# The last eleven slots of a fused attention and expert kernel, written out by hand over three bank pairs

## What is computed

```python
q = xn @ Wq + bq;  latent = xn @ Wl + bl          # 16 heads of 8
k = latent @ Wk + bk;  v = latent @ Wv + bv
attn = softmax(q k^T / sqrt(8))                    # per head, 256 x 256
y_attn = (attn v) @ Wo + bo

f = batchnorm(xn @ fWq + fbq)                      # 8 heads of 32 = two halves of 16
s0, s1 = l2norm(half) . l2norm(sub_key)            # 32 scores for each half
ts0, ti0 = top4(s0);  ts1, ti1 = top4(s1)
w = softmax of the 16 sums ts0[i] + ts1[j];  expert = 32*ti0 + ti1   # clamped to 128 experts
y_ffn = sum_k up[expert_k] * w_k * gelu(down[expert_k] . xn)
out = x + y_attn + y_ffn
```

## Time and profile before

| | |
|---|---|
| median of 3 runs | 374.73 us (374.39 to 374.91) |
| the profiled execution | 377.74 us, its span 375.7 us |
| busy over the span: PE, DVE, ACT, POOL | 327.1, 329.2, 254.1, 255.1 us |
| mean granted TensorE clock | 0.968 |
| first second scores after slot 127, start | 344.21 us |
| last copy to ysb, start | 373.02 us |

### The profile page before, as it was taken

How to read it: one execution, slowest core, us unless ns; L and a number is a source line. 1 busy time by engine, 2 the same in 40 slices (tenths; PEclk the granted TensorE clock), 3 DMA queues, 4 the chain that set the end, 5 groups by cost and what they waited for, 6 DMA issues and landing times.

```text
span 375.7 us, 9660 instructions
## 1 busy us (share of the span) xinstructions
PE 327.1 (87%) x3080; PEld 175.1 (47%) x3080; DVE 329.2 (88%) x1407; ACT 254.1 (68%) x388; POOL 255.1 (68%) x544
## 2 busy tenths in 40 slices
PE   3999897976998898989898989898998989898874
PEld 2455553342354454544454545454454544454443
DVE  6599988789779999999999999999999999998561
ACT  3699967867566757667666676766757667667761
POOL 6388876706656777685867767677777675857870
PEclk9999996996599999999999999999999999999999
DMA  4664676029140403242141505050403130000100
GB/s 133 180 182 134 182 177 165 7 58 100 26 77 17 72 26 77 55 49 73 30 87 18 90 12 101 4 100 16 87 25 77 54 50 19 1 17 3 31 16 14
DMA packets 45886, 24.81 MB, mean 66 GB/s; under 512 B 5452, under 2 KB 45708, under 8 KB 45836
## 3 DMA queue, kind: packets, MB, share of 16 engines
q1 hardware_dynamic: 45836, 24.20, 30.3%
HBM read 15.54 MB, written 8.39 MB: 64 GB/s over the span
## 4 chain that ended last, share of the span: by engine, by line
PE 55%; DVE 24%; issue 8%; ACT 8%; POOL 4%; POOLq 0%; ACTq 0%; DVEq 0%
PE bank L590 12%; DVE negm L820 9%; PE bank L650 8%; PE bank L633 8%; PE SI L526 7%; DVE r_sb L885 6%; PE SJ L569 5%; PE SJ L607 2%; ACT s_sb L380 2%; PE bank L675 2%; POOL prod L1038 2%; PE bank L677 2%; PE bank L676 2%; PE bank L539 1%; PE SI L454 1%
## 5 line engine op out<-in xcount | busy, mean ns | idle before, releaser
L820 DVE TENSOR_REDUCE negm<-SI 128x4 f32<-128x1024 f32 x128 | 154.2, 1216 | 5.2 <-PE SI L526 5.0
L413 ACT ACTIVATE Eb<-SJ 128x1024 f32<-128x1024 f32 x128 | 130.6, 1020 | 32.3 <-PE SJ L569 32.2
L1038 POOL TENSOR_TENSOR prod<-r_sb,a 128x1024 f32<-128x1024 f32 x31 | 60.2, 1943 | 26.6 <-issue 25.8
L590 PE MATMUL bank<-Eb,vhat 128*18 128x256 f32 x1024 | 70.3, 394 | 0.0
L526 PE MATMUL SI<-KS,QS 48*128 48x256 bf16 x512 | 51.8, 281 | 15.5 <-DVE negm L820 14.6
L569 PE MATMUL SJ<-QS,KS 50*128 50x256 bf16 x512 | 51.7, 282 | 8.2 <-ACT Eb L413 8.0
L865 DVE MAX8 top<-s_sb 128x8 f32<-128x32 f32 x512 | 50.6, 180 | 4.9 <-ACT s_sb L380 4.9
L526 PEld LDWEIGHTS SI<-KS,QS 48*128 48x128 bf16 x512 | 18.2, 96 | 55.3 <-issue 43.5
L885 DVE MATCH_REPLACE8 r_sb<-top,s_sb 128x36 f32<-128x36 f32 x256 | 43.1, 180 | 0.0
L650 PE MATMUL bank<-cst,prod 128*128 128x128 f32 x256 | 34.5, 278 | 4.2 <-ACT s_sb L380 3.5
L633 PE MATMUL bank<-kblk,fqT 128*128 128x256 f32 x128 | 37.1, 413 | 0.5 <-ACT s_sb L380 0.4
(11 more groups left out here) (144 smaller groups left out, 585.9 us busy)
## 6 DMA issues: line engine op xcount, KB each, us to landing
qk_parts<-parts SPq DMA_DIRECT2D x48, 128.0 KB, 2.4
QS<-qk_parts SPq DMA_DIRECT2D x32, 96.0 KB
KS<-qk_parts SPq DMA_DIRECT2D x32, 96.0 KB
x_sb<-L_attn_x SPq DMA_DIRECT2D x8, 256.0 KB, 3.4
QS<-qk_parts SPq DMA_DIRECT2D x32, 64.0 KB
KS<-qk_parts SPq DMA_DIRECT2D x32, 64.0 KB
out<-ysb SPq DMA_DIRECT2D x16, 128.0 KB, 2.8
QS<-qk_parts SPq DMA_DIRECT2D x32, 32.0 KB
```

The lines of the kernel that those rows point to most:

```text
L413: A(Eb[:, n % 4, :], SJ[:, :], ACT.Exp).then_inc(s["ex"], 1)
L590: last = mm(psO[32 * c:32 * c + 2 * VC, (q % 2) * S:(q % 2 + 1) * S], vhat[:, v0:v0 + 2 * VC], Eb[:, (2 * g + c // 2) % 4, e0:e0 + S], sta ...
L820: V.tensor_reduce(negm[:, bb % 2, :, :, pr].rearrange("p t e -> p e t"), SI[slot % 2][:, :].rearrange("p (e t j) -> p e t j", e=2, j=S), a ...
L1038: TT(prod[:, t, :, :, :], r_sb[:, hs, 0:NK].unsqueeze(2).to_broadcast([P, FH, TOP, NK]), a0[:, hs, :].unsqueeze(3).to_broadcast([P, FH, TO ...
```

## The change

Slots 0 to 127 stay as they are, but for one memset. NSLOT becomes 128, and each engine's block gets its remaining work written out after the loop, with N0 = 117 (second scores left: 117 to 127) and LB = 15:

- `second(n)`: second scores rotate over SJ, SI1 and SI0, which the first scores have left. Their wait is then for exp n - 2.
- the expert scores of batch 15 go first, into the two halves of SI0 (`psS`), both tiles together, and ScalarE copies them to `s_last`, a view of the start of fqT, in place of `s_sb`. Its padding is set by the memset of slot 68.
- batch 15's ranks are made on VectorE, not GpSimd, and so are both halves of its products.
- its products, outputs and heads are turned into SI0 and SI1 (`psT`, `psC`, `psP`), and its last projection goes into SJ (`psY`), where the wgT and x matmuls are issued before the turned heads, and only Wo by onT after.
- values that open a half of `psO` from pair 116 on wait for the copy of the other half too (`o_ev` one higher).

```diff
+        s_last = fqT[:, 0, 0:NH * 2 * KP].rearrange("p (h a k) -> p h a k", a=2, k=KP)
+        wgT_last = fqT[:, 1, 0:S]
...
+        psS = [SI[0][:, 0:512], SI[0][:, 512:1024]]
+        psT, psC, psP = SI[0][:, 0:S], SI[1][:, 0:512], SI[0][:, 512:512 + S]
+        psY = SJ[:, :].rearrange("p (t z) -> p t z", t=2)[:, :, 0:D]
...
-        NSLOT = NPAIR * B + LAG + 6
+        NSLOT = NPAIR * B
+        N0 = NSLOT - LAG
+        LB = B - 1
+        def second(n):
+            return SJ if n <= N0 else (SJ, SI[1], SI[0])[(n - N0) % 3]
...
+            finished(LB - 2, in_bank)
+            act.wait_ge(s["pad2"], 1)
+            last_scores(0)
+            weights(N0)
+            act.wait_ge(s["mt"], B)
+            act.wait_ge(s["mrow"], 32 * LB)
+            A(mT[:, :], psM[0:2 * H, 0:S], ACT.Copy).then_inc(s["mt_ev"], 1)
+            last_scores(1)
+            weights(N0 + 1)
+            outputs(2 * LB - 2)
+            for n in range(N0 + 2, N0 + 5):
+                weights(n)
+            outputs(2 * LB - 1)
+            weights(N0 + 5)
...
+                elif n <= N0:
+                    pe.wait_ge(s["ex"], n)
+                elif n == N0 + 1:
+                    pe.wait_ge(s["mx"], NSLOT)
+                elif n == N0 + 2:
+                    pe.wait_ge(s["fs_ev"], 2 * B)
+                else:
+                    pe.wait_ge(s["ex"], n - 2)
...
+                    pe.wait_ge(s["o_ev"], q if 2 * g >= N0 - 1 else q - 1)
...
+            pe.wait_ge(s["mx"], NSLOT - 1)
+            pe.wait_ge(s["ff"], B)
+            for t in range(BT):
+                scores(LB, t, psS[t])
+            sj(N0)
+            turn_maxima(LB)
+            values(4 * LB - 3)
+            sj(N0 + 1)
+            sj(N0 + 2)
+            values(4 * LB - 2)
...
+            pe.wait_ge(s["ex"], N0 + 9)
+            pe.wait_ge(s["last_pr"], 2)
+            turn_products(0, psT)
+            values(4 * LB + 3)
+            pe.wait_ge(s["last_pr"], 4)
+            turn_products(1, psT)
+            turn_outputs(LB, psC)
+            for t in range(BT):
+                mm(psY[:, t, :], wgT_last[:, t * P:(t + 1) * P], up_sb[:, :], start=True, stop=False)
+                mm(psY[:, t, :], ident, x_sb[:, BT * LB + t, :], start=False, stop=False)
+            turn_heads(LB, psP)
+            pe.wait_ge(s["onT"], B)
+            for t in range(BT):
+                last = mm(psY[:, t, :], onT[:, t * P:(t + 1) * P], wo_sb[:, :], start=False, stop=True)
...
+            dve.wait_ge(s["y"], LB - 1)
+            gated(LB - 1, psM[:, 0:S], wgT)
...
+            V.tensor_scalar(rank[:, 1, :, :], rank[:, 0, :, :], float(TOP), None, ALU.is_lt).then_inc(s["sel"], 1)
+            second_half(LB)
...
+            normalised(LB - 1, psM)
+            dve.wait_ge(s["fa"], B)
+            dve.wait_ge(s["es"], B)
+            dve.wait_ge(s["wt"], 2 * LB)
+            for t in range(2):
+                hs = slice(FH * t, FH * (t + 1))
+                V.tensor_tensor(prod[:, t, :, :, :], r_sb[:, hs, 0:NK].unsqueeze(2).to_broadcast([P, FH, TOP, NK]),
+                                a0[:, hs, :].unsqueeze(3).to_broadcast([P, FH, TOP, NK]), ALU.mult).then_inc(s["last_pr"], 1)
...
+                if slot == 68:
+                    pool.wait_ge(s["fs"], 10)
+                    V.memset(s_last[:, :, :, NK:KP], NEG).then_inc(s["pad2"], 1)
```

More of the change, by code:

```diff
@@ L555, in _ @@
                 n = slot - LAG
[L556 to L572, removed]
-                m = slot - LAG - 3
[L574 to L593, removed]
+                if n >= 0:
+                    sj(n)
+                m = slot - LAG - 3
+                if m >= 0 and m % 2 == 0:
+                    values(m // 2)
                 if slot < NPAIR * B - 1:
@@ L613, in _ @@
                 if k == 0 and 0 <= b < B:
[L614 to L620, removed]
+                    turn_maxima(b)
                 if k in (1, 2) and 0 <= b < B:
-                    t = k - 1
-                    if b == 0 and t == 0:
+                    if b == 0 and k == 1:
                         pe.wait_ge(s["kblk"], 1)
-                    if t == 0:
+                    if k == 1:
                         pe.wait_ge(s["mt_ev"], b + 1)
@@ L630, in _ @@
                         pe.wait_ge(s["fs_ev"], 2 * b + 1)
[L631 to L635, removed]
+                    scores(b, k - 1, psM)
                 b = (slot - LAG - 8) // 8
@@ L649, in _ @@
[L649 to L652, removed]
+                        pe.wait_ge(s["fs_ev"], 2 * (b + 2))
+                    turn_products(t, psM)
                 b = (slot - LAG - 10) // 8
                 if k == 5 and 0 <= b < B:
-                    pe.wait_ge(s["o_ev"], 2 * (b + 1))
@@ L657, in _ @@
[L657 to L661, removed]
+                    turn_outputs(b, psM)
                 b = (slot - LAG - 11) // 8
                 if k == 6 and 0 <= b < B:
-                    pe.wait_ge(s["on"], b + 1)
-                    for t in range(BT):
-                        last = turn(psM[:, t * P:(t + 1) * P], on[:, t, :], ident)
@@ L667, in _ @@
-                    last.then_inc(s["onp"], 1)
+                    turn_heads(b, psM)
                 b = (slot - LAG - 12) // 8
                 if k == 7 and 0 <= b < B:
-                    pe.wait_ge(s["onT"], b + 1)
                     if b == 0:
                         pe.wait_ge(s["xb"], 4)
[L674 to L677, removed]
@@ L681, in _ @@
+            for t in range(BT):
+                last = mm(psY[:, t, :], onT[:, t * P:(t + 1) * P], wo_sb[:, :], start=False, stop=True)
+            last.then_inc(s["y"], 1)
         @block.vector
@@ new lines, in _ @@
+            for t in range(2):
+                dve.wait_ge(s["t4"], 2 * LB + t + 1)
+                dve.wait_ge(s["pr"], 4 * LB - 2 * (1 - t))
+                for h in range(FH * t, FH * (t + 1)):
+                    last = V.match_replace(r_sb[:, h, :], top4[:, h, :], s_last[:, h, 1, :], NEG)
+                last.then_inc(s["mr"], 2)
+            dve.wait_ge(s["y"], LB - 1)
+            gated(LB - 1, psM[:, 0:S], wgT)
+            first = s_last[:, :, 0, 0:TOP]
+            best = top8[:, :, 0, 0:TOP]
```

245 lines of the change are left out of this document (223 added, 22 removed).

## The result

| | before | changed |
|---|---|---|
| median, 19 runs each | 374.94 us | 371.10 us (369.0 to 373.89) |
| ratio, 95% interval | | 0.991 (0.9885 to 0.9935) |
| profiled execution, span | 377.74, 375.7 us | 370.48, 368.7 us |
| tail | 30.35 us | 26.58 us |

A forecast was written before the change was run, and what follows sets the result against it. Batch 15's ranks and products were taken to set the end. Four queues walked forward gave wgT 1.97 us earlier plus 0.89 less 0.02 behind it: 2.84 us off, 371.9 us; range 371.3 to 372.6, 8 in 10 371.0 to 373.4.

The forecast's parts named there:

- values 58 waiting 0.87 us: TensorE in the tail: values 58 wait for ScalarE's psO copy behind exp 118, starting 0.87 us after the queue is free.
- second scores 120 not waiting for the max rows: Tail: max rows arrive by 351.44 at the latest, 0.4 us before second scores 120 want them; wait taken as nothing.
- The head lost: Start of the tail: expert scores go first, so second scores 117 start at 346.33 instead of 344.21 us.
- the middle won: Second scores 120 to 122, values 59 and second products follow without gap, 351.84 to 354.84 us, no longer waiting for each exp.
- Expert scores of both tiles go first, 2 x 1.06 us: TensorE at the tail's start: batch 15's expert scores precede second scores 117, at 1.06 us for each tile.
- 3 x 0.33: TensorE mid-tail: second scores 120 to 122 priced at 0.33 us each, start to start.
- I take 2.6: Batch 15's 12 rank instructions on VectorE: 2.6 us taken, 3.3 the upper end, against 4.81 on GpSimd.
- My line through two-input rows: VectorE instruction price for the ranks: 0.16 us plus 1.04 ns per element, from rows of 2 and 1024 elements.
- the shortened chain: Rival: the rank chain is shorter and TensorE alone bounds; saving 3.4 us or slightly more, time 371.3; chance 0.12.
- the ranks on VectorE are the term that decides: Batch 15's ranks before batch 14's normalisation: VectorE holds TensorE 0.87 us; chain length goes straight through, down by at most 0.5.
- the last batch's ranks and products set the end: Kernel before, end: VectorE and GpSimd shut each other out, so batch 15's ranks and products fix the final copy at 373.02.
- The memset of slot 68: In the loop, waiting on expert scores done 26 slots earlier: costed at nothing, some 0.2 us if uncovered.

The follow-up runs named there:

- e3: Changed kernel with the 12 rank instructions of batch 15 back on GpSimd behind z; tail 26.40 us against 26.58.
- e2: Changed kernel without the rotation, second scores 118 to 127 all to SJ; tail 30.76 us against 26.58, ratio to the kernel before 0.998.
- e1: Changed kernel with the wgT and x matmuls of the last projection behind the turned heads again; tail 27.49 us against 26.58.
- e4: Changed kernel with the first half of batch 15's product and its add back on GpSimd; tail 27.04 us against 26.58.
- e7: Changed kernel with ScalarE's psO copy for values 58 moved ahead of exp 118; tail 25.82 us against 26.58.
- e9: Changed kernel with psO copy ahead of exp 118 and batch 14's normalisation ahead of r_sb, den, dinv; tail 25.45 us against 26.58.
- e5: Kernel before plus only the rotation of second scores 118 to 127, with the higher o_ev wait; tail 32.89 us against 30.35.
- e11: Rotation alone on the kernel before, run again; tail 30.24 us; six runs 372.89 to 374.79 us, four 378.97 to 379.56.
- e12: Rotation alone plus four unread expert-score matmuls in TensorE's wait for the last products; tail 30.23 us, run medians 374.25 and 376.55.
- e6: Kernel before with only batch 15's 12 rank instructions on VectorE, ahead of batch 14's wgT; tail 31.41 us against 30.35.

## Why the prediction was right, and where it was off

The forecast was 371.9 us, the measured median 371.1: just below the forecast's own range of 371.3 to 372.6, and inside the wider one from 371.0. The queues moved as walked, step by step: second scores 117 late, values 58 waiting 0.87 us (0.87 forecast), second scores 120 not waiting for the max rows, the products of batch 15 off TensorE's path, the clock at 1.00, and 0.90 us saved behind wgT (0.87 forecast). The head lost and the middle won as walked. What did not hold is the reading of what decides, below.

The size was off by 0.93 us, 3.77 against 2.84, in the price of steps that I had taken from neighbours of another kind:
- "Expert scores of both tiles go first, 2 x 1.06 us": 1.82, so 0.30 less. If the first tile still costs 1.06, the second, right behind it in another bank, costs 0.76.
- "3 x 0.33" for second scores 120 to 122: 0.76, so 0.23 less.
- "I take 2.6" for the ranks: 2.44 where the walk had 2.61, so 0.17 less. My line through two-input rows (0.43 us for 256 elements) does not hold for instructions with one input: that comparison took 0.28. The Trainium skill's section on mode 2x_2P in "VectorE: DVE Perf Modes" was the source of the estimate that I set beside the sum, 0.17 us less for the two comparisons; the 0.28 us agrees with it.
- the projection of batch 13, taken as 1.54, has 1.44 with the scores behind it (0.10), and the first products of batch 15 0.96 instead of 1.03 (0.07). The last 0.06 are spread over steps.

Of the rivals, the shortened chain ("saving 3.4 or slightly more, time 371.3") came closest in time, in part by luck: the rank chain was only 0.17 us shorter, and TensorE alone does not bound; it still waited 0.74 us for VectorE. Most of its size came from TensorE steps that I had priced too high.

One reading fell with e3: "the ranks on VectorE are the term that decides". They lie on the path, but moving them there is not where the gain comes from. With it falls part of the opening reading, that "the last batch's ranks and products set the end": e2 has both off GpSimd and is no faster than the kernel before. The gain comes from the rotation together with an order that uses it: 4.18 us are lost without the rotation (e2), 0.91 without the early matmuls (e1), 0.46 with the first half of the product back on GpSimd (e4), and 0.18 are gained with the ranks back there (e3). These don't add up to 3.77. A likely reason, which no run tests alone, is that the order puts 1.82 us of expert scores at the front, which the rotation makes up for. That the number still came out follows from the sum being a walk over all four queues, rotation included, and not a price for the ranks.

"The memset of slot 68" at nothing held. It runs for 0.20 us at 217.23 us, and the changed kernel's row maxima are 3.25 us ahead of those of the kernel before both in front of it (200.32 against 203.57) and at the end of the loop (336.34 against 339.60, 3.26). Why executions come in two kinds of clock near 90 to 105 us stays open.

## What to carry to other kernels

Where the end of a kernel is a relay between in-order queues, walk the queues forward with start-to-start steps: the walks for e1 to e4 and e7 to e9, made when the changed kernel's steps were known, met their tails within 0.2 us, and so did that for e5's kernel where the clock stayed up (e11, e12). The first walk, with steps taken from other neighbours, was 0.93 us off, and the walk for e6, which left out GpSimd beside the ranks, 1.4. The parts of such a change have no worth of their own: the rotation, without which 4.18 us are lost, gains 0.1 us alone and loses 2.5 in some executions, and the ranks on VectorE, which cost 0.18 us in the whole, cost 1.06 alone. And a stage that frees TensorE early can leave a wait behind which it loses its clock in some executions, so look at the longest single wait that a change leaves, and not only at the sum.

## What the runs showed of the hardware that I had not expected

- In e5 a wait of 2.11 us on TensorE was followed by a granted clock of 0.51; by their mean clock (0.957) 5 of the 11 executions of this kernel did so. The same wait in e11, and one of 2.15 us in e6, left it at 1.00. Why is open.
- A comparison with a constant, f32 in SBUF, ran at 0.28 us for 256 elements where a subtraction took 0.41, and one of 96 elements, 0.20 us alone, lasted 1.06 beside a GpSimd instruction (e6), although it reads one tensor only.
- VectorE's add of 8 elements beside a GpSimd product lasted 1.76 to 1.77 us in four kernels (before, e4, e12, and that of e5 and e11), 0.17 to 0.18 with GpSimd idle.
- Who is slowed turned with who started first. In e4 VectorE's product starts 0.10 us ahead and takes its usual 1.23 us, GpSimd's takes 2.89 where it has 1.91 elsewhere. In e6 GpSimd's starts 0.32 us ahead and takes 1.91, VectorE's takes 2.67.
